# Order of the first loads, of the weight splits and of the position network at the start of a two-layer transformer kernel

## What is computed

```python
xn = ln(x, g_norm)
q = (xn @ Wq).reshape(b, n, HEADS, DIM_HEAD).transpose(0, 2, 1, 3)
kv = xn @ Wkv
k, v = (kv[..., :DIM_HEAD], kv[..., DIM_HEAD:])
...
q = l2norm(q) * q_scale
k = l2norm(k) * k_scale
sim = jnp.einsum('bhid,bjd->bhij', q, k) * SCALE
bias = rel_pos_bias(n, w0, b0, g0, w1, b1, g1, w2, b2, q.dtype)
```

## Time and profile before

| | us |
|---|---|
| median of three runs | 1526.59 (1524.34 to 1528.87) |
| profiled execution | 1527.73 |
| its span, first to last instruction | 1526.0 |
| TensorE busy in it | 1349.5 (88%) |
| VectorE busy | 1127.1 (74%) |
| ScalarE busy | 893.8 (59%) |
| GpSimd busy | 795.6 (52%) |

### The profile page before, as it was taken

How to read it: one execution, slowest core, us unless ns; L and a number is a source line. 1 busy time by engine, 2 the same in 40 slices (tenths; PEclk the granted TensorE clock), 3 DMA queues, 4 the chain that set the end, 5 groups by cost and what they waited for, 6 DMA issues and landing times.

```text
span 1526.0 us, 43298 instructions
## 1 busy us (share of the span) xinstructions
PE 1349.5 (88%) x15534; PEld 1178.9 (77%) x15535; DVE 1127.1 (74%) x2218; ACT 893.8 (59%) x2229; POOL 795.6 (52%) x838
## 2 busy tenths in 40 slices
PE   1889999999759999979999999768998867999993
PEld 0778988889648999868888888547787756888883
DVE  4488888888844556689999999748886797545457
ACT  1457767667527666746665666437786544545556
POOL 1256656665505545555555555358884023777740
PEclk9899999999979999999999999979997989999997
DMA  7210000000011000000000000110003203233318
GB/s 203 33 36 8 9 8 8 10 8 9 33 30 53 1 0 0 1 9 9 9 7 9 9 9 8 26 48 15 14 14 111 74 1 121 93 101 99 96 43 331
DMA packets 82391, 65.09 MB, mean 43 GB/s; under 512 B 50734, under 2 KB 76081, under 8 KB 81202
## 3 DMA queue, kind: packets, MB, share of 16 engines
q1 hardware_dynamic: 75314, 44.98, 10.3%
q0 software_dynamic: 6912, 17.84, 3.7%
HBM read 39.18 MB, written 18.35 MB: 38 GB/s over the span
## 4 chain that ended last, share of the span: by engine, by line
PE 75%; DVE 10%; issue 6%; ACT 5%; POOL 2%; SPq 1%; DMA 1%; DVEq 0%; ACTq 0%; POOLq 0%
PE psW L1968 12%; PE psQ L1889 12%; PE psQ L2261 8%; PE psW L2240 4%; PE psS L1950 4%; PE psS L1993 4%; PE psT L1926 3%; PE psQ L2062 3%; PE psW L2050 3%; PE psM L2050 3%; PE psS L2062 3%; PE psM L1937 2%; PE psT L2229 1%; PE psM L1907 1%; PE psT L2248 1%
## 5 line engine op out<-in xcount | busy, mean ns | idle before, releaser
L732 POOL TENSOR_TENSOR pn<-ex,rden 128x1024 f32<-128x1024 f32 x64 | 144.0, 2250 | 245.3 <-PE psT L1926 240.7
L1889 PEld LDWEIGHTS psQ<-xT,wq 128*128 128x128 f32 x1536 | 201.1, 200 | 46.0 <-issue 24.1
L1968 PE MATMUL psW<-wout,oT 128*128 128x256 f32 x1536 | 210.3, 292 | 16.4 <-ACT oT L963 14.4
L1889 PE MATMUL psQ<-xT,wq 128*128 128x256 f32 x1536 | 220.9, 297 | 1.5 <-ACT cur L1044 1.5
L1968 PEld LDWEIGHTS psW<-wout,oT 128*128 128x128 f32 x1536 | 195.3, 194 | 29.3 <-ACT oT L963 24.0
L2261 PE MATMUL psQ<-W,exT 128*128 (+1 forms) x624 | 173.8, 414 | 0.0
L777 POOL TENSOR_TENSOR hT<-hf,hT 128x512 fp32r<-128x512 f32 x64 | 84.4, 1318 | 99.9 <-ACT hT L1040 99.9
L2261 PEld LDWEIGHTS psQ<-W,exT 128*128 128x128 f32 x624 | 112.2, 193 | 19.2
L2240 PE MATMUL psW<-W,ehT 128*128 (+1 forms) x624 | 103.4, 303 | 8.3 <-DVE ehT L1803 8.2
L1347 DVE SCALAR_TENSOR_TENSOR oT<-psS,nvcol,oT 128x512 fp32r<-128x512 f32 x128 | 89.7, 740 | 23.8 <-ACT oT L963 23.2
L1320 DVE TENSOR_TENSOR ex<-ex,m 128x1040 f32<-128x1040 f32 x64 | 103.6, 1619 | 2.2
(11 more groups left out here) (310 smaller groups left out, 3477.3 us busy)
## 6 DMA issues: line engine op xcount, KB each, us to landing
both<-results SPq DMA_DIRECT2D x8, 1024.0 KB, 13.3
raw_w<-W SPq DMA_DIRECT2D x27, 256.0 KB, 4.2
vv<-vp SPq DMA_DIRECT2D x256, 16.0 KB, 1.8
xf<-xf_all SPq DMA_DIRECT2D x4, 1024.0 KB
out<-X SPq DMA_DIRECT2D x8, 512.0 KB, 5.0
X<-x SPq DMA_DIRECT2D x1, 3584.0 KB, 14.3
raw_q<-Wq SPq DMA_DIRECT2D x2, 1024.0 KB, 6.0
bvv<-v_all SPq DMA_DIRECT2D x128, 16.0 KB, 1.8
```

Of the source, the lines that this page charges most:

```text
L732: nc.gpsimd.tensor_tensor(pn[:], ex[t % 2][:, :, 0:S], rden[:].unsqueeze(2).to_broadcast([P, H, S]), ALU.mult).then_inc(sem("t_pn"), 1)
L1889: mm = nc.tensor.matmul(psQ[:, cc, h * QT:h * QT + QT], wq[w][:, k, c * P:c * P + P], xT[g % 2][u][:, k, :], start=(k == 0 and j == 0), st ...
L1968: mm = nc.tensor.matmul(psW[:, 0:D], oT[u][:, c, :], wout[w][:, c, :], start=(u == 0 and c == 0 and w == 0), stop=(u == 1 and c == CH - 1))
```

## The change

- Loads. On SyncE, layer 0 only: after X's first tiles and gcol comes Wq, as the third load, into a buffer of its own, `first_q`, in a part of the output buffer O that is written much later; then raw_kvn, the network's b1, g1, w2, b2, the null values and null bias; then the 28 tiles of X, then the masks and Wout. On ScalarE, as its first instructions, eleven loads: w0, b0, g0, w1, nkb, ksrow, qsrow and the four pieces of ksc and qsc. gcol and Wq count on f_loaded (two), masks and Wout on d_loaded (five), 13 loads are left on l_loaded.
- Splits. The query weights are split first, right after the first two tiles, and TensorE's first query bank waits for them alone; the key/value weights are split at the end of step -1, and the key/value product of tile 0 waits for them. Wout's high half is made at the end of step 0, its low half at the end of step 1, the masks at the end of step 0. In layer 1 the query weights are split before the key/value weights too.
- Position network. VectorE runs its first layer ahead of the null key and with the query weights' low halves between its pieces, its second layer between the null key's products; TensorE makes its first product between the two first query banks and the rest at the end of step -1, into another bank of PSUM.
- GpSimd writes the causal mask in step 2, behind rq of tile 0.

The waits of later loads on f_loaded and d_loaded are raised by 32 and 80. The core of the diff:

```diff
+        first_q = nc.alloc_sbuf_tensor_at("first_q", [P, KD, INNER], F32, offset=rp + 24 * K)
...
+        def load_rel(eng, rows, ends):
+            for name, key in rows:
+                eng.dma_start(r_rows[name][:], a[key].rearrange("(o d) -> o d", o=1).to_broadcast([P, D])).then_inc(sem("rel_loaded"), 16)
+            if ends:
+                eng.dma_start(r_w2[:], a["rw2"].rearrange("(k p) n -> p k n", p=P)).then_inc(sem("rel_loaded"), 16)
+                eng.dma_start(r_b2[:], a["rb2"].rearrange("(h o) -> h o", o=1), allow_slow_non_contiguous=True).then_inc(sem("rel_loaded"), 16)
...
-                sp.dma_start(gcol[:], a[L["g"]].rearrange("(k p) -> p k", p=P), allow_slow_non_contiguous=True).then_inc(ld, 16)
-                sp.dma_start(nkb[:], a["null"][0:1, :].to_broadcast([P, DH])).then_inc(ld, 16)
+                first = sem("f_loaded") if L["cosine"] else ld
+                last = sem("d_loaded") if L["cosine"] else ld
+                load_q = lambda: sp.dma_start(given_q(L)[:], a[L["wq"]].rearrange("(k p) n -> p k n", p=P)).then_inc(first, 16)
+                sp.dma_start(gcol[:], a[L["g"]].rearrange("(k p) -> p k", p=P), allow_slow_non_contiguous=True).then_inc(first, 16)
+                if L["cosine"]:
+                    load_q()
+                    sp.dma_start(raw_kvn[:, :, 0:2 * DH], a[L["wkv"]].rearrange("(k p) n -> p k n", p=P)).then_inc(ld, 16)
+                    load_rel(sp, (("b1", "rb1"), ("g1", "rg1")), True)
+                else:
+                    sp.dma_start(nkb[:], a["null"][0:1, :].to_broadcast([P, DH])).then_inc(ld, 16)
...
+                if L["cosine"]:
+                    sp.dma_start(X[:, 4:TILES, :], x_dram[:, 4:TILES, :]).then_inc(sem("x_in1"), 16)
...
-                            sp.dma_start(mask_w[row:row + S // 2, :, :], seq.to_broadcast([S // 2, TILES, S // 4])).then_inc(ld, 16)
+                            sp.dma_start(mask_w[row:row + S // 2, :, :], seq.to_broadcast([S // 2, TILES, S // 4])).then_inc(last, 16)
...
-                sp.dma_start(raw_q[:], a[L["wq"]].rearrange("(k p) n -> p k n", p=P)).then_inc(ld, 16)
-                sp.dma_start(raw_kvn[:, :, 0:2 * DH], a[L["wkv"]].rearrange("(k p) n -> p k n", p=P)).then_inc(ld, 16)
-                sp.dma_start(raw_o[:], a[L["wo"]].rearrange("(k p) n -> p k n", p=P)).then_inc(ld, 16)
+                if not L["cosine"]:
+                    load_q()
+                    sp.dma_start(raw_kvn[:, :, 0:2 * DH], a[L["wkv"]].rearrange("(k p) n -> p k n", p=P)).then_inc(ld, 16)
+                sp.dma_start(raw_o[:], a[L["wo"]].rearrange("(k p) n -> p k n", p=P)).then_inc(last, 16)
...
-            for half in range(2):
-                for row, name in ((ksc, "k_scale"), (qsc, "q_scale")):
-                    sp.dma_start(row[half * DH:(half + 1) * DH, :], a[name].rearrange("(d o) -> d o", o=1),
-                                 allow_slow_non_contiguous=True).then_inc(sem("l_loaded"), 16)
...
-            pool.wait_ge(sem("nk_turn"), 1)
-            nc.gpsimd.tensor_tensor(tiny[:, 2:3], tiny[:, 1:2], mhalf[:, 0:1], ALU.pow).then_inc(sem("nk_turn"), 1)
...
                 if L["cosine"]:
-                    pool.wait_ge(sem("t_rk"), 1)
+                    pool.wait_ge(sem("t_rstd"), 6)
+                    pool.wait_ge(sem("t_rk"), 2)
+                    pool.wait_ge(sem("t_rq"), 1)
                 else:
...
             rel_rstd(0)
+            pool.wait_ge(sem("nk_turn"), 1)
+            nc.gpsimd.tensor_tensor(tiny[:, 2:3], tiny[:, 1:2], mhalf[:, 0:1], ALU.pow).then_inc(sem("nk_turn"), 1)
...
-                    if t == 0:
+                    if t == (1 if L["cosine"] else 0):
...
         @block.scalar
         def _(act):
+            load_rel(act, (("w0", "rw0"), ("b0", "rb0"), ("g0", "rg0")), False)
+            act.dma_start(r_w1[:], a["rw1"].rearrange("(k p) n -> p k n", p=P)).then_inc(sem("rel_loaded"), 16)
+            act.dma_start(nkb[:], a["null"][0:1, :].to_broadcast([P, DH])).then_inc(sem("l_loaded"), 16)
+            for row, name in ((ksrow, "k_scale"), (qsrow, "q_scale")):
+                act.dma_start(row[:], a[name].rearrange("(o d) -> o d", o=1).to_broadcast([P, DH])).then_inc(sem("l_loaded"), 16)
+            for half in range(2):
+                for row, name in ((ksc, "k_scale"), (qsc, "q_scale")):
+                    act.dma_start(row[half * DH:(half + 1) * DH, :], a[name].rearrange("(d o) -> d o", o=1),
+                                  allow_slow_non_contiguous=True).then_inc(sem("l_loaded"), 16)
...
                 norm_hi(0, t)
-            split_hi(LAYERS[0])
+            act.wait_ge(sem("f_loaded"), FIRST_LOADS)
             for k in range(KD):
-                split_q_hi(k)
...
             def second_layer(i):
-                if i == -4:
+                if i == -1:
                     rel_silu(1)
-                elif i == -3:
                     rel_transposed(1)
                     act.wait_ge(sem("rel_turn"), 5 + REL["mm"])
-                    nc.scalar.activation(r_out[:], psW[0:H, 0:P], ACT.Identity, bias=r_b2[:, 0:1]).then_inc(sem("rel_turn"), 1)
+                    nc.scalar.activation(r_out[:], psS[0:H, 1, 0:P], ACT.Identity, bias=r_b2[:, 0:1]).then_inc(sem("rel_turn"), 1)
+                    split_hi(LAYERS[0])
+                elif i == 0:
+                    act.wait_ge(sem("d_loaded"), LAST_LOADS)
                     split_out_hi()
                 elif i == TILES - 2:
...
+                if not L["cosine"]:
+                    for k in range(KD):
+                        null_product(L, k)
+                        null_scores(L, k)
+            def null_product(L, k):
+                if k:
+                    dve.wait_ge(sem("l_wn"), nth(L, "wn", k))
+                nc.vector.tensor_tensor(wn_tmp[:], given_q(L)[:, k, :].rearrange("p (h d) -> p h d", h=H),
+                                        nkb[:].unsqueeze(1).to_broadcast([P, H, DH]), ALU.mult).then_inc(sem("l_nk"), 1)
...
+            def null_scores(L, k):
+                dve.wait_ge(sem("l_nk"), nth(L, "nk", (7 if L["cosine"] else 2) + k))
+                nc.vector.tensor_reduce(raw_kvn[:, k, 2 * DH:KVN], wn_tmp[:], AX.X, ALU.add).then_inc(sem("l_wn"), 1)
+            def split_q_lo(L, k):
+                dve.wait_ge(sem("l_whi"), nth(L, "whi", k + 1))
+                nc.vector.scalar_tensor_tensor(wq[1][:, k, :], given_q(L)[:, k, :], gcol[:, k:k + 1],
+                                               wq[0][:, k, :].bitcast(F32), ALU.mult, ALU.subtract).then_inc(sem("l_wlo"), 1)
+            def split_kvn_lo(L, k):
+                dve.wait_ge(sem("l_whi"), nth(L, "whi", KD + k + 1))
+                nc.vector.scalar_tensor_tensor(wkvn[1][:, k, :], raw_kvn[:, k, :], gcol[:, k:k + 1],
+                                               wkvn[0][:, k, :].bitcast(F32), ALU.mult, ALU.subtract).then_inc(sem("l_wlo"), 1)
...
+                if L["cosine"]:
+                    dve.wait_ge(sem("d_loaded"), LAST_LOADS)
...
-            def rel_norm(k, src):
+            def rel_moments(k, src):
                 c = sem("rel_chain")
                 nc.vector.bn_stats(r_st[:], src).then_inc(c, 1)
                 dve.wait_ge(c, 4 * k + 2)
                 nc.vector.bn_aggr(r_mv[:], r_st[:]).then_inc(sem("rel_mv"), 1)
+            def rel_scaled(k, src):
+                c = sem("rel_chain")
                 dve.wait_ge(sem("rel_rstd"), 2 * k + 2)
                 nc.vector.tensor_scalar(r_h[:], src, r_mv[:, 0:1], r_rs[:, 1:2], ALU.subtract, ALU.mult).then_inc(c, 1)
...
-                    norm_apply(done, i + 3)
-                    if live(i + 4):
-                        start(i + 4)
-                    norm_stats(done, i + 4)
-                    norm_moments(done, i + 4)
+                    if i >= 0 or not L["cosine"]:
+                        norm_apply(done, i + 3)
+                        if live(i + 4):
+                            start(i + 4)
+                        norm_stats(done, i + 4)
+                        norm_moments(done, i + 4)
...
-            split_lo(LAYERS[0])
+            rel_moments(0, r_h[:])
+            split_q_lo(LAYERS[0], 0)
+            rel_scaled(0, r_h[:])
+            split_q_lo(LAYERS[0], 1)
+            norm_apply(0, 2)
+            norm_stats(0, 3)
+            norm_moments(0, 3)
+            null_key(LAYERS[0])
+            null_product(LAYERS[0], 0)
+            null_scores(LAYERS[0], 0)
+            dve.wait_ge(sem("rel_turn"), REL["mm"])
+            nc.vector.tensor_tensor(r_h[:], psS[:, 0, 0:D], r_rows["b1"][:], ALU.add).then_inc(sem("rel_chain"), 2)
+            dve.wait_ge(sem("rel_chain"), 5)
+            rel_moments(1, r_h[:])
+            null_product(LAYERS[0], 1)
+            rel_scaled(1, r_h[:])
+            null_scores(LAYERS[0], 1)
...
-                if i == -4:
-                    dve.wait_ge(sem("rel_turn"), REL["mm"])
```

(31 more changed lines are left out.)

66 lines of the change are left out of this document (21 added, 45 removed).

## The result

The changed kernel takes 1522.74 us (median of 7 runs, 1519.58 to 1524.44) against 1528.19 (7 runs) for the kernel before: a ratio of 0.9972 (0.9959 to 0.9984), 5.5 us less where 18.5 were forecast. Its profiled execution took 1524.44 with a span of 1522.6.

A forecast was written before the change was run, and what follows sets the result against it. The prediction took TensorE to bound the long part, so time could be had only ahead of it: 20.0 us at the first key/value product, less 0.3 and 1.2 in the loop, 18.5, giving 1508.1 us; forecast 1505 to 1511, bounds 1502.5 to 1516.

The forecast's parts named there:

- both query banks in the shadow: Start: moving 9 us of TensorE work, query banks and network product, costs nothing while VectorE's chain is this long.
- The high half of Wout and the masks: Step 0: Wout's high half on ScalarE costs 0.3 us (ends 0 and 1.9); masks on VectorE cost nothing, uncovered 1.2.
- Rival C: Loop: Wout and masks, issued last, land late and stall ScalarE and VectorE; slower than before, 1530 at 60 us; chance 0.03.
- The step that failed: Start: b2 lands by 13.5 at the latest, so VectorE's first network step was taken at 12.0.
- Rival A: Start: loads later and ScalarE's issues dearer, 3 us together, plus 2.7 for Wout's halves: 1513; chance 0.13.
- the signs named for being wrong: VectorE waiting for a load past 14, query matmuls waiting for the network, or first-to-fifth product distance over 2 us longer.
- The second step: Loop, behind step 1: Wout's low half on VectorE delays GpSimd's rq(1) and costs 1.2 us, ends 0 and 2.3.
- Nothing: Loop: the causal mask behind rq(0) fits GpSimd's idle 7.61 us and costs nothing.
- the third sign: Loop: the distance from the first key/value product to the fifth is over 2 us longer than before.
- rival D: Later stages: the gain is given back as another start shifts which TensorE waits have a lower clock behind them; chance 0.03.

The follow-up runs named there:

- e6: Changed kernel with only w0, b0, g0 and w1 on ScalarE's queue, the other seven small loads back on SyncE's; ratio 0.9941 to the kernel before.
- e1: Changed kernel with all first loads on SyncE's queue, the network's eight directly behind Wkv; ratio 0.9952 to the kernel before.
- e3: Changed kernel with Wq's low halves ahead of the wait for the network's loads and the first query bank ahead of its transposes; ratio 0.9954 to the kernel before.
- e2: Changed kernel with the masks moved to the end of step -1 and Wout's low half to the end of step 0; ratio 0.9956 to the kernel before.
- e5: Changed kernel with one queue in the order the work asks for loads, masks at the end of step -1, Wout's low half at step 0's; ratio 0.9901 to before.
- e10: Second set of runs of the one-queue kernel with reordered loads and masks and Wout's low half earlier; 1511.63 against 1529.11 us before, ratio 0.9879.

## Why the prediction was wrong

**What was right.** What bounds the start, and what the new order does to it. From VectorE's first network step to the product of tile 0 the forecast had 17.5 us, measured were 18.7: null key 2.1 (2.0), a product and a reduction 2.5 (2.5), TensorE's product done 0.6 before VectorE comes, both query banks in the shadow. The high half of Wout and the masks cost nothing (0.3 and 0 forecast): kT of tile 0 waited 0.24 for TensorE, not for Wout's high half, and came 9.9 us behind the product of tile 0 (10.0 before). The order of the work by itself is worth 12.3 us at tile 0. Rival C did not happen, but with less room than priced: the rest of X went out at 11.40 instead of 8.6, SyncE needed 20.24 us for the masks' four issues behind it, and Wout landed at 37.8 instead of by 31; it was asked for at 47.4. Had the product of tile 0 come at the forecast 29.5, Wout would have been asked for some 10.1 us earlier, at 37.3 (an estimate), and that is 0.5 before it landed.

**The step that failed** is the first one: "so b2 goes out at 5.0; with the 8.5 us that rows of 128 KB took to land behind large loads it is there at 13.5, the high end". It went out at 6.17, since issues of two engines at a time took up to 1.2 us each, and landed after 14.7. 20.9 for 12.0 is 8.9 of the 10.1 us by which the product of tile 0 came late. I gave small loads the time of the bytes ahead of them ("fewer bytes than before"), and took for the second queue only its share of the bandwidth, 2 us on the first X load. That 2 us was right: the first X load took 6.1 instead of 4.1, and the tiles were done at 12.7. Rival A named the loads, with 3 us in all where 8.9 came. What held them up was seven small loads on ScalarE's queue: e6, which moves only those behind b2, has the first network step at 13.27, and e1, without the second queue, at 12.87. How they hold it up is shown only in part (the equal packet counts from 8 to 13 us). The earlier trace rows had a hint: qsrow, 32 KB, took 7.25 us to land, as long as loads many times its size. The upper bound should have counted the small loads on both queues. Two of the signs named for being wrong came with it: VectorE waited for a load past 14, and the query matmuls waited for the network, at 26.2 instead of 16 to 17; e3, where they don't, starts them at 15.84 and gains 3.4 us at tile 0.

**The second step** is a mis-sized term: Wout's low half, forecast 1.2 through GpSimd's rq(1) (ends 0 and 2.3), cost 2.7 by the fifth product (43.0 us behind the first, 40.3 before), above its upper end. The path was another one, too: VectorE's own list, which runs without a gap up to its first score, and not rq(1). I had moved the causal mask behind rq(0) and priced it "Nothing", and had Wout's low half beside it without asking whether the two slow each other: alone 2.35 and 2.29, together 4.29 and 2.87. e2 gives it back in full (40.3). This is the third sign that the forecast named, a distance over 2 us longer.

**The third** is rival D, with 0.03: part of the gain is given back later, 2.5 to 4.6 us. I had weighed it only at the 14 us that would undo the gain ("No row says that it comes to 14 us"), and not at the 3 us that three runs spread over 4.5 could have suggested.

The sum again, from the first traces: 9.8 us at the product of tile 0 instead of 20.0; less 2.8 to tile 6 (1.5 forecast) are 7.1; 7.8 at tile 31; 5.5 in the time. The range, 1502.5 to 1516, was built on a bound of 13.5 for b2 that no row limited from above. The kernel with the loads in the right order and Wout's low half a step earlier, e5 and e10 at 1512.5 and 1511.6, lies inside it, though not at 1508.1 nor within 1505 to 1511. It is another kernel, so this does not save the forecast.

## What to carry to other kernels

Count small loads, not only their bytes: in the slow stretches here each of them (a row of 256 bytes to 128 partitions, a column of 4-byte elements) cost about a microsecond, in others 0.3. So put those that the first wait asks for first, and count the others on another semaphore. A second queue is cheap while it is short (0.4 us at the first network step with four loads); with seven small loads more it delayed the load that was waited for by 7.6 us. When work is moved under an idle engine, ask what runs on VectorE and GpSimd in the same microseconds, and trace a kernel twice before reading a difference of 2 us from its clock.

## What the runs showed of the hardware

- Two queues of loads moved equal numbers of packets from 8 to 13 us (246 to 245, 302 to 297, 55 to 56), and unequal ones from 14 to 20 (1272 to 415). A load of 0.1 KB was there 14.7 us after its issue beside eleven loads on the second queue, after 5.8 in a single queue.
- Mostly columns of 4-byte elements and rows of 256 bytes spread over 128 partitions moved at 200 to 280 packets in 2 us (e1, 12 to 16 us), at 8 to 13% of the engines' time, where larger packets (0.62 MB in 723) filled the engines at 8 to 10 us. In the kernel before 2524 packets of under 512 bytes moved in 2 us.
- An issue on ScalarE's queue took 0.45 to 1.20 us (11 of them 0.80 to 8.96), on SyncE's in the same time 0.45 to 1.23.
- VectorE's pass over Wout and GpSimd's causal mask took 2.87 and 4.29 us side by side, 2.29 and 2.35 apart.
- The clock granted to TensorE differed between executions of one kernel, 0.950 to 0.960 in 38 of the kernel before, with times from 1522.9 to 1531.9 us.
